# Gather indices four groups ahead and four buffers of gathered rows in the last layer's edge loop

## The chip, the cores and the metric

The program runs on one core of a Trainium2 chip. The metric is the device time of one execution in microseconds (us), the median of several runs. The core has five engines with an instruction queue each: PE (TensorE, matrix products), DVE (VectorE), ACT (ScalarE), POOL (GpSimd, which here issues the indirect transfers) and SP (SyncE, which issues plain transfers). They meet through semaphores: an instruction raises one when it has finished, another queue waits until it has reached a value.

## The reference

Four graph layers run on 3125 nodes of 256 features with 53125 edges: an attention layer, a message-passing layer of five rounds, a mean over neighbours, and last the layer that the change touches (`_L3_gnn_ref`):

```python
row, col = (edge_indices[0], edge_indices[1])
edge_in = jnp.concatenate([h[row], h[col], edge_attr], axis=-1)
msg = jax.nn.relu(edge_in @ W1.T + b1) @ W2.T + b2
agg = jax.ops.segment_sum(msg, row, num_segments=h.shape[0])
...
h_new = (1.0 - z) * n + z * h
```

The kernel splits `W1` by columns: one part multiplies `h[row]`, one `h[col]`, one the edge attributes. The first two are made once for each node, so that for an edge only a sum of three terms is left, a ReLU, and a sum over the edges of a node (`W2` is folded into later weights).

## The kernel before

The last layer's edge loop works on groups of 4 x 128 edges; `GL = SL // 4` = 110 groups. Edges are sorted by source node, so the source term of a group comes by one-hot products from `row_parts` in SBUF. The `col` term comes from DRAM: `col_dram` holds one row of 256 floats for each node, and POOL gathers 128 rows with each of four `indirect_dma_start` (L2100), whose indices stand in `m_idx`. Groups alternate between two halves of each buffer (q = 0 and 1): `m_idx`, `col_rows`, `m_msg`, `p_pre`, `m_hotT`, `attrT`. `m_ends` and `m_attrs` have four slots and come by SP from `rec_dram`.

What each queue does for group g, in the order of the code:

- SP, `load_over(g)` (L2080): waits for the index copy, the local numbers and the turned attributes of group g - 4, then issues the two loads (L2075, L2076).
- DVE, `work(g)`: `choose(g + 2)` (local numbers L2206, one-hots `turn_hot` L2211); `sum_parts(g + 1)` (L2219 on: waits for the rows of g + 1, `rows_in`, and for PE's `pre_done`; two adds L2223 of `col_rows` and `p_pre` into `m_msg`; raises `pre_added`); `add_sums(g)` (four adds of `p_sum` into `agg_sum` L2232, between them `sum_hot` of the next group L2215).
- PE, in a pair: `products(g + 1)` (L2128 and L2132 into `p_pre`, raises `pre_done`), `turn(g + 2)` (transposes L2117, raises `attrT_ps`, and L2121), `add_up(g)` (L2143 into `p_sum`, waits for ACT's `msg_ready`).
- ACT: `finish(g)` (ReLU L2181, waits for `pre_added`), then `prepare(g + 2)`: the index copy L2171, the copy of `attrT` L2175, which waits for PE's `attrT_ps` and `pre_done`, and the copy of `m_hotT` L2177.
- POOL, `gather(g + 2)`: waits for that index copy (`idx_ready`) and for `sum_parts(g)` (`pre_added`), whose buffer it writes over.

The queues are written out by hand, with no scheduler. The order of each is the order of the calls.

Of the kernel before, what the change touches and what calls it, by code (L numbers as in the profile page):

```python
# [9 lines left out]
I32 = mybir.dt.int32  # L10
# [120 lines left out]
def program(nc, a, out):  # L131
# [9 lines left out]
    with top:  # L141
        def sb(name, shape, dt, ctx=top):
            return ctx.enter_context(nc.sbuf_tensor(name, shape, dt))
# [1795 lines left out]
        with ExitStack() as ctx:  # L1939
# [9 lines left out]
            with ExitStack() as inner:  # L1949
# [93 lines left out]
                idx = [sb(f"m_idx{q}", [P, 4], I32, inner) for q in range(2)]  # L2043
                col_rows = [sb(f"col_rows{q}", [P, 4, D], F32, inner) for q in range(2)]
# [14 lines left out]
                rows_in = [sem(f"e_rows_in{q}") for q in range(2)]  # L2059
# [9 lines left out]
                with nc.Block() as block:  # L2069
# [23 lines left out]
                    @block.gpsimd  # L2093
                    def _(pool):
                        def gather(g, q):
                            pool.wait_ge(idx_ready, g + 3)
                            pool.wait_ge(pre_added, g + 1)
                            pool.nop().then_inc(waits_passed, 1)
                            for u in range(4):
                                nc.gpsimd.indirect_dma_start(  # L2100
                                    col_rows[q][:, u, :], None, col_dram,
                                    bass.IndirectOffsetOnAxis(ap=idx[q][:, u:u + 1].bitcast(U32), axis=0)).then_inc(rows_in[q], 16)

                        def pair_of(i):
                            gather(i * 2, 0)
                            gather(i * 2 + 1, 1)
                        looped(pool, GL // 2, pair_of)
# [56 lines left out]
                    def _(act):  # L2164
                        act.nop().then_inc(idx_ready, 2)

                        def prepare(g, q, i, slot, n):
                            act.wait_ge(ends_in[slot], n * 16 + 16)
                            if i is not None:
                                act.wait_ge(rows_in[q], i * 64)  # L2170
                            nc.scalar.copy(idx[q][:], ends[slot][:, :, 0:1].rearrange("p u o -> p (u o)")).then_inc(idx_ready, 1)  # L2171
                            act.wait_ge(attrT_ps, g + 3)
                            if i is not None:
                                act.wait_ge(pre_done, g - 1)
                            nc.scalar.copy(attrT[q][:], p_attrT[:])  # L2175
                            act.wait_ge(hotT_ps, g + 1)
                            nc.scalar.copy(hotT[q][:], p_hotT[:]).then_inc(turned_sb, 1)  # L2177
# [5 lines left out]
                        def pair_of(i, slot, n):  # L2183
                            finish(i * 2, 0)
                            prepare(i * 2 + 2, 0, i + 1, slot, n)
                            finish(i * 2 + 1, 1)
                            prepare(i * 2 + 3, 1, i + 1, slot + 1, n)

                        prepare(0, 0, None, 0, 0)
                        prepare(1, 1, None, 1, 0)  # L2190
                        two_pairs(act, pair_of)
# [4 lines left out]
                    def _(dve):  # L2196
# [20 lines left out]
                        def sum_parts(g, q, i):  # L2217
                            dve.wait_ge(rows_in[q], i * 64 + 64)
# [3 lines left out]
                            for v in range(2):  # L2222
                                r = TT(msg[q][:, 2 * v:2 * v + 2, :], col_rows[q][:, 2 * v:2 * v + 2, :], p_pre[q][:, 2 * v:2 * v + 2, :], ALU.add)  # L2223
# [14 lines left out]
                        def work(g, q, i, tiles, slot, n):  # L2238
                            choose(g + 2, q, i + 1, slot, n)
                            sum_parts(g + 1, 1 - q, i + q)  # L2240
# [12 lines left out]
                        sum_parts(0, 0, 0)  # L2253
                        two_pairs(dve, pair_of)
                        tiles = read_registers(nc, by_src_table, SL - 8, 8, ET.DVE, NT - 1)
                        sum_parts(GL - 1, 1, GL // 2 - 1)
# [200 lines left out]
```

## Time and profile before

| | |
|---|---|
| median of 3 runs | 4330.24 us (4321.47 to 4361.82) |
| profiled execution, its time | 4346.08 us |
| profiled execution, its span | 4344.2 us |
| last layer's edge loop, first load to last add | 3346.67 to 4173.15 us of the span |
| PE busy there (3366 to 4157 us) | 631.09 of 791.00 us |
| DVE, ACT, POOL busy there | 487.86, 217.66, 405.43 us |
| mean granted TensorE clock over the span | 0.859 |

Busy time is the sum of an engine's instructions without those that only wait, move registers or issue plain transfers. The execution's own time lies 1.88 us over its span, and the profiled execution 15.84 us over the median of the three runs.

### The profile page before, as it was taken

Reading aid. Unit: us, or ns where it says so; the run is one execution under the profiler, and the core shown is the slowest. Engines: PE = TensorE matmul, PEld = TensorE weight load, DVE = VectorE, ACT = ScalarE, POOL = GpSimd, SP = SyncE. Lnnn points to the kernel's source line nnn. Section 1 sums busy time; section 2 is a strip of 40 time slices with the busy share of each in tenths; the row PEclk is TensorE's granted clock in tenths of the full one; section 3 lists DMA queues with packets and bytes.
Section 4 is the critical chain, followed back from the end, with each engine's and each line's share of the span. In section 5 each row is a group of like instructions: output and inputs, shape, how many; then the busy total and the mean of one; then the engine's idle time right before and its main releaser. Section 6 shows DMA issues by size and latency. Waiting matters only on the chain. (4 is left out here: it accounts for less than half of the span.)

```text
span 4344.2 us, 64735 instructions
## 1 busy us (share of the span) xinstructions
PE 3493.5 (80%) x16068; PEld 2303.3 (53%) x16069; DVE 2472.1 (57%) x7800; ACT 1066.5 (25%) x2559; POOL 2135.9 (49%) x1867
## 2 busy tenths in 40 slices
PE   6377777777887777669898989897896888787878
PEld 4245555555655555435454555554555555455544
DVE  8756777777777777662222222213555666566668
ACT  0121222222222222132121222211544222222222
POOL 0366788787888888304444444420001555545510
PEclk9877777777777777779999999998898999999989
DMA  7258565665555556223434444431232333333320
GB/s 255 45 136 283 133 136 132 135 135 132 137 133 138 137 134 138 53 70 125 157 115 154 130 134 135 134 104 47 74 118 57 93 92 88 88 87 89 89 59 21
DMA packets 490706, 505.18 MB, mean 116 GB/s; under 512 B 225327, under 2 KB 395789, under 8 KB 490523
## 3 DMA queue, kind: packets, MB, share of 16 engines
q0 software_dynamic: 141664, 236.21, 22.7%
q1 hardware_dynamic: 336238, 248.00, 20.0%
q10 hardware_dynamic: 12749, 20.33, 1.3%
q8 instruction: 23, 0.38, 0.0%
q14 instruction: 32, 0.26, 0.0%
HBM read 433.87 MB, written 70.48 MB: 116 GB/s over the span
## 5 line engine op out<-in xcount | busy, mean ns | idle before, releaser
L1039 PE MATMUL p_out<-rows,hot 128*128 128x266 f32 x2048 | 828.6, 559 | 33.0 <-DVE rows L1161 25.6
L964 POOL DMA_INDIRECT count_dram<-number,place x384 | 653.8, 1703 | 164.7 <-issue 121.2
L1573 POOL DMA_INDIRECT rec_dram<-records,edge_place x416 | 408.4, 982 | 515.1 <-PE p_hi L1615 232.6
L1039 PEld LDWEIGHTS p_out<-rows,hot 128*128 128x128 f32 x2048 | 522.7, 275 | 229.3 <-DVE rows L1161 104.6
L2100 POOL DMA_INDIRECT col_rows<-col_dram,m_idx x440 | 417.9, 950 | 454.3 <-ACT m_idx L2171 313.9
L956 POOL DMA_INDIRECT rows<-att_dram,idx x512 | 550.6, 1075 | 163.3 <-issue 139.9
L1503 PE MATMUL p_hi<-cbuf,parts 128*128 128x400 f16 x1750 | 582.7, 333 | 2.9 <-issue 2.8
L1502 PE MATMUL p_lo<-cbuf,parts 128*128 128x400 f16 x1750 | 583.2, 333 | 2.3 <-issue 2.3
L1531 DVE TENSOR_TENSOR node_sum<-p_hi,low_sb 128x400 f32<-128x400 f32 x80 | 46.0, 574 | 656.1 <-ACT low_sb L1522 623.9
L1161 DVE TENSOR_TENSOR rows<-rows 128x512 f32<-128x512 f32 x512 | 351.1, 686 | 0.2 <-ACT rows L930 0.2
L1022 PE MATMUL p_top<-rhs,hot 128*128 128x17 f32 x1024 | 185.3, 318 | 174.1 <-DVE rhs L1100 159.6
L2128 PE MATMUL p_pre<-attr_w,attrT 128*128 128x512 f32 x440 | 242.4, 634 | 45.4 <-ACT m_hotT L2177 45.4
L1022 PEld LDWEIGHTS p_top<-rhs,hot 128*128 128x128 f32 x1024 | 172.0, 254 | 192.7 <-DVE rhs L1100 176.5
L2232 DVE TENSOR_TENSOR agg_sum<-agg_sum,p_sum 128x256 f32 x440 | 185.1, 421 | 151.9 <-remote 78.0
L1502 PEld LDWEIGHTS p_lo<-cbuf,parts 128*128 128x128 f16 x1750 | 171.4, 98 | 148.1 <-issue 23.3
L907 ACT COPY scores<-rows 128x64 f32<-128x64 f32 x128 | 39.3, 307 | 855.3 <-DMA rows<-att_dram,idx 855.3
L2143 PE MATMUL p_sum<-m_msg,sum_hot 128*128 128x256 f32 x880 | 244.1, 426 | 4.1 <-DVE sum_hot L2215 4.1
L1503 PEld LDWEIGHTS p_hi<-cbuf,parts 128*128 128x128 f16 x1750 | 171.5, 98 | 132.2 <-issue 13.0
L2132 PEld LDWEIGHTS p_pre<-row_parts,m_hotT 128*128 128x128 bf16 x1320 | 132.9, 101 | 147.9 <-issue 135.7
L2223 DVE TENSOR_TENSOR m_msg<-col_rows,p_pre 128x512 f32<-128x512 f32 x220 | 141.2, 683 | 119.9 <-remote 52.6
L1522 ACT ACTIVATE low_sb<-p_lo 128x400 f32<-128x400 f32 x80 | 40.3, 504 | 650.8 <-PE p_hi L1504 603.5
L1978 POOL MEMSET attr_w<- 128x512 f32 x1 | 0.5, 525 | 399.0 <-POOLq L365 399.0
(394 smaller groups left out, 6247.5 us busy)
## 6 DMA issues: line engine op xcount, KB each, us to landing
cbuf<-count_dram SPq DMA_DIRECT2D x40, 2500.0 KB
dl_rep<-dl_dram SPq DMA_DIRECT2D x128, 256.0 KB
count_dram<-zeros SPq DMA_DIRECT2D x20, 1000.0 KB, 21.2
g_rows<-count_dram SPq DMA_DIRECT2D x25, 800.0 KB, 4.2
rec_dram<-blank ACTq DMA_DIRECT2D x1, 17600.0 KB
records<-in_edges POOLq DMA_DIRECT2D x32, 520.0 KB
key_rep<-key_dram SPq DMA_DIRECT2D x64, 256.0 KB
m_attrs<-rec_dram SPq DMA_DIRECT2D x110, 128.0 KB
```

What stands on the lines that cost most here:

```text
L956: nc.gpsimd.indirect_dma_start(rows[r][:, u, :], None, att_dram, bass.IndirectOffsetOnAxis(ap=idx[r][:, u:u + 1].bitcast(U32), axis=0)).th ...
L964: nc.gpsimd.indirect_dma_start(count_dram, bass.IndirectOffsetOnAxis(ap=place[r][:, n, c:c + 1].bitcast(U32), axis=0), number[r][:, 2 * n ...
L1022: m = nc.tensor.matmul(p_top[:, u, :], hot[r][:, u, :], rhs[:, u, :], start=True, stop=True)
L1039: m = nc.tensor.matmul(p_out[q][:, side, 0:HALF], hot[k][:, u, :], rows[k][:, u, side * HALF:(side + 1) * HALF], start=(u == 0), stop=(u = ...
L1161: TT(row[:, :, 0:HEAD - 1], row[:, :, 0:HEAD - 1], row[:, :, HEAD - 1:].broadcast_to([P, HW, HEAD - 1]), ALU.mult).then_inc(msg_ready, 1)
L1502: nc.tensor.matmul(p_lo[m][:], parts[:, k, m, 1, :], cbuf[q][:, k, :], start=(k == 0), stop=(k == NT - 1))
L1503: nc.tensor.matmul(p_hi[m][:], parts[:, k, m, 0, :], cbuf[q][:, k, :], start=(k == 0), stop=False)
L1573: nc.gpsimd.indirect_dma_start(rec_dram, bass.IndirectOffsetOnAxis(ap=edge_place[:, at:at + 1].bitcast(U32), axis=0), records[b % 3][:, j, ...
L2100: nc.gpsimd.indirect_dma_start(col_rows[q][:, u, :], None, col_dram, bass.IndirectOffsetOnAxis(ap=idx[q][:, u:u + 1].bitcast(U32), axis=0) ...
L2128: nc.tensor.matmul(p_pre[q][:, 2 * v:2 * v + 2, :].rearrange("p u d -> p (u d)"), attrT[q][:, v, :], attr_w[:].rearrange("p k d -> p (k d) ...
L2143: r = nc.tensor.matmul(p_sum[v][:, u, :], sum_hot[q][:, 2 * v + u, :], msg[q][:, 2 * v + u, :], start=True, stop=True)
L2232: TT(own, own, p_sum[u // 2][:, u % 2, :], ALU.add).then_inc(added, 1)
```

## The change

ACT no longer makes the indices of group g + 2 within `prepare(g + 2)`. A new function `index` makes them from four buffers: four at the start, and from then on two at the head of each pair, those of groups g + 4 and g + 5, before `finish(g)`. POOL's `gather(g + 4)` waits for its indices and for `sum_parts(g)`; `col_rows` and `m_idx` have four buffers, with a semaphore for each of the four. DVE's `sum_parts` reads the buffer of its slot. PE and SP keep their queues.

```diff
-                idx = [sb(f"m_idx{q}", [P, 4], I32, inner) for q in range(2)]
-                col_rows = [sb(f"col_rows{q}", [P, 4, D], F32, inner) for q in range(2)]
+                idx = [sb(f"m_idx{q}", [P, 4], I32, inner) for q in range(4)]
+                col_rows = [sb(f"col_rows{q}", [P, 4, D], F32, inner) for q in range(4)]
...
-                rows_in = [sem(f"e_rows_in{q}") for q in range(2)]
+                rows_in = [sem(f"e_rows_in{q}") for q in range(4)]
...
-                        def gather(g, q):
-                            pool.wait_ge(idx_ready, g + 3)
-                            pool.wait_ge(pre_added, g + 1)
-                            pool.nop().then_inc(waits_passed, 1)
+                        def gather(g, slot):
...
+                        def gather_over(g, slot):
+                            pool.wait_ge(idx_ready, g + 3)
+                            pool.wait_ge(pre_added, g - 1)
+                            pool.nop().then_inc(waits_passed, 1)
+                            gather(g, slot)
+
+                        for g in range(4):
+                            pool.wait_ge(idx_ready, g + 3)
+                            gather(g, g)
...
-                        def prepare(g, q, i, slot, n):
+                        def index(slot, n, fresh=False):
                             act.wait_ge(ends_in[slot], n * 16 + 16)
-                            if i is not None:
-                                act.wait_ge(rows_in[q], i * 64)
-                            nc.scalar.copy(idx[q][:], ends[slot][:, :, 0:1].rearrange("p u o -> p (u o)")).then_inc(idx_ready, 1)
+                            if not fresh:
+                                act.wait_ge(rows_in[slot], n * 64)
+                            nc.scalar.copy(idx[slot][:], ends[slot][:, :, 0:1].rearrange("p u o -> p (u o)")).then_inc(idx_ready, 1)
+
+                        def prepare(g, q, i):
...
-                        def pair_of(i, slot, n):
+                        def pair_of(i):
                             finish(i * 2, 0)
-                            prepare(i * 2 + 2, 0, i + 1, slot, n)
+                            prepare(i * 2 + 2, 0, i + 1)
...
+                        def both(j):
+                            for half in range(2):
+                                index(2 * half, j + 1)
+                                index(2 * half + 1, j + 1)
+                                pair_of(j * 2 + half)
...
-                        def sum_parts(g, q, i):
-                            dve.wait_ge(rows_in[q], i * 64 + 64)
+                        def sum_parts(g, q, slot, n):
+                            dve.wait_ge(rows_in[slot], n * 64 + 64)
```

On ACT, in the loop's body, the order of one pair before (the branch and the register rows are the sequencer's; L2181 is the ReLU, L2171 the index copy):

```order
L2181 ACTIVATE m_msg<-m_msg 128x1024
L2168 ISA
L2170 ISA
L2171 COPY m_idx<-m_ends 128x4
L2172 REGISTER_ALU
L2174 REGISTER_ALU
L2175 COPY attrT<-p_attrT 128x256
L2177 COPY m_hotT<-p_hotT 128x512
L2180 REGISTER_ALU
L2181 ACTIVATE m_msg<-m_msg 128x1024
L2171 COPY m_idx<-m_ends 128x4
```

The same place on ACT after (L2178 is now the index copy, L2190 the ReLU, L2184 and L2186 the copies of `attrT` and `m_hotT`):

```order
L2177 REGISTER_ALU
L2178 COPY m_idx<-m_ends 128x4 x2
L2189 ISA
L2190 ACTIVATE m_msg<-m_msg 128x1024
L2181 REGISTER_ALU
L2183 REGISTER_ALU
L2184 COPY attrT<-p_attrT 128x256
L2186 COPY m_hotT<-p_hotT 128x512
L2189 REGISTER_ALU
L2190 ACTIVATE m_msg<-m_msg 128x1024
```

Two index copies stand together ahead of the pair's first ReLU, where one stood behind each ReLU.

On POOL, from the start of the block through the loop before (each `x4` is one group's four gathers):

```order
L2100 DMA col_rows<-col_dram,m_idx 128x256 x8
L115 UNCONDITIONAL_BRANCH
L115 ISA
L2097 REGISTER_ALU
L2100 DMA col_rows<-col_dram,m_idx 128x256 x4
L2096 REGISTER_ALU
L2097 REGISTER_ALU
L2100 DMA col_rows<-col_dram,m_idx 128x256 x4
```

and after:

```order
L2097 DMA col_rows<-col_dram,m_idx 128x256 x16
L2110 UNCONDITIONAL_BRANCH
L2110 ISA
L2103 REGISTER_ALU
L2097 DMA col_rows<-col_dram,m_idx 128x256 x4
L2102 REGISTER_ALU
L2097 DMA col_rows<-col_dram,m_idx 128x256 x4
```

Four groups are gathered before the loop instead of two; the loop then gathers one group at a time, as before, four ahead of the sum that frees its buffer.

## Rows read from the trace of the kernel before

**Rows 1.** The page, head, section 1 and groups of section 5

```profile
span 4344.2 us, 64735 instructions
...
PE 3493.5 (80%) x16068; PEld 2303.3 (53%) x16069; DVE 2472.1 (57%) x7800; ACT 1066.5 (25%) x2559; POOL 2135.9 (49%) x1867
...
L2100 POOL DMA_INDIRECT col_rows<-col_dram,m_idx x440 | 417.9, 950 | 454.3 <-ACT m_idx L2171 313.9
```

**Rows 2.** Busy time of each engine in three stretches of the edge loop

```profile
core 0: us, PE busy (x) PEld busy (x) DVE busy (x) ACT busy (x) POOL busy (x), PEclk, DMA share, GB/s
3349.00:3366.00 17.00, 10.74 (x41) 5.92 (x42) 4.33 (x20) 3.05 (x7) 9.60 (x10) 0.73 0.51 111
3366.00:4157.00 791.00, 631.09 (x3218) 427.18 (x3215) 487.86 (x1605) 217.66 (x429) 405.43 (x428) 0.94 0.36 89
```

**Rows 3.** Line L2175, ACT's copy of attrT: what ended its waits

```profile
L2175 ACT COPY attrT<-p_attrT x110: 372/373/374, 3350.4 to 4156.9; 128x256 f32<-128x256 f32 x110
its engine sat idle before it (us, times) until:
  DMA g_rows<-count_dram: 313.8, 43
  PE p_attrT L2117: 168.1, 56
```

**Rows 4.** Timeline of ACT, one pair of groups

```profile
3712.09 0.37 ACT L2175 COPY attrT<-p_attrT 128x256 f32<-128x256 f32 x1 [7.65 <-DMA g_rows<-count_dram]
...
3713.46 1.06 ACT L2181 ACTIVATE m_msg<-m_msg 128x1024 f32<-128x1024 f32 x1 [0.52 <-DVE m_msg L2223]
3714.43 0.18 ACT L2171 COPY m_idx<-m_ends 128x4 int32<-128x4 int32 x1
...
3718.72 1.06 ACT L2181 ACTIVATE m_msg<-m_msg 128x1024 f32<-128x1024 f32 x1
3719.69 0.18 ACT L2171 COPY m_idx<-m_ends 128x4 int32<-128x4 int32 x1
3727.03 0.37 ACT L2175 COPY attrT<-p_attrT 128x256 f32<-128x256 f32 x1 [7.16 <-DMA g_rows<-count_dram]
```

**Rows 5.** Timeline of POOL, the same pair

```profile
3715.46 0.95 POOL L2100 DMA_INDIRECT col_rows<-col_dram,m_idx  x1 [5.32 <-ACT m_idx L2171]
...
3720.72 0.96 POOL L2100 DMA_INDIRECT col_rows<-col_dram,m_idx  x1 [0.56 <-issue]
...
3724.49 0.95 POOL L2100 DMA_INDIRECT col_rows<-col_dram,m_idx  x1 [0.31 <-issue]
```

**Rows 6.** Timeline of the same pair: PE, DVE and SP

```profile
3712.14 1.29 DVE L2223 TENSOR_TENSOR m_msg<-col_rows,p_pre 128x512 f32<-128x512 f32 x2 [3.20 <-PE p_sum L2143]
...
3717.41 1.28 DVE L2223 TENSOR_TENSOR m_msg<-col_rows,p_pre 128x512 f32<-128x512 f32 x2
...
3722.24 0.82 PE L2132 MATMUL p_pre<-row_parts,m_hotT 128*128 x6
...
3723.33 1.95 PE L2143 MATMUL p_sum<-m_msg,sum_hot 128*128 128x256 f32 x8
...
3727.08 1.29 DVE L2223 TENSOR_TENSOR m_msg<-col_rows,p_pre 128x512 f32<-128x512 f32 x2 [4.09 <-remote]
3727.25 0.37 SPq L2075 DMA_DIRECT2D m_ends<-rec_dram  x1
```

**Rows 7.** Timeline, a pair whose first gather was followed by a pause

```profile
3757.16 1.28 DVE L2223 TENSOR_TENSOR m_msg<-col_rows,p_pre 128x512 f32<-128x512 f32 x2 [4.22 <-remote]
...
3763.66 0.95 POOL L2100 DMA_INDIRECT col_rows<-col_dram,m_idx  x1 [2.23 <-issue]
...
3771.18 0.95 POOL L2100 DMA_INDIRECT col_rows<-col_dram,m_idx  x1 [0.30 <-issue]
...
3773.76 1.28 DVE L2223 TENSOR_TENSOR m_msg<-col_rows,p_pre 128x512 f32<-128x512 f32 x2 [5.95 <-remote]
```

**Rows 8.** Timeline of a pair without the long wait, ACT and POOL

```profile
3434.00 1.06 ACT L2181 ACTIVATE m_msg<-m_msg 128x1024 f32<-128x1024 f32 x1
...
3436.01 0.95 POOL L2100 DMA_INDIRECT col_rows<-col_dram,m_idx  x1 [1.20 <-issue]
...
3446.66 1.06 ACT L2181 ACTIVATE m_msg<-m_msg 128x1024 f32<-128x1024 f32 x1
```

**Rows 9.** Timeline at the start of the loop: the first load and index copy

```profile
3346.67 0.37 SPq L2075 DMA_DIRECT2D m_ends<-rec_dram  x1
...
3348.59 0.19 ACT L2171 COPY m_idx<-m_ends 128x4 int32<-128x4 int32 x1 [4.16 <-DMA m_ends<-rec_dram]
```

More of the change, by code:

```diff
@@ L2094, in _ @@
                     def _(pool):
-                        def gather(g, q):
-                            pool.wait_ge(idx_ready, g + 3)
-                            pool.wait_ge(pre_added, g + 1)
-                            pool.nop().then_inc(waits_passed, 1)
+                        def gather(g, slot):
                             for u in range(4):
                                 nc.gpsimd.indirect_dma_start(
[L2101 to L2107, printed above, removed]
+                                    col_rows[slot][:, u, :], None, col_dram,
+                                    bass.IndirectOffsetOnAxis(ap=idx[slot][:, u:u + 1].bitcast(U32), axis=0)).then_inc(rows_in[slot], 16)
+                        def gather_over(g, slot):
[6 more added lines that the diff above has]
+                            gather(g, g)
+                        with pool.Fori(1, GL // 4) as j:
+                            for slot in range(4):
+                                gather_over(j * 4 + slot, slot)
+                        for g in range(GL // 4 * 4, GL):
+                            gather_over(g, g % 4)
                     @block.tensor
@@ L2181, in finish @@
                             nc.scalar.activation(msg[q][:], msg[q][:], ACT.Relu).then_inc(msg_ready, 1)
-                        def pair_of(i, slot, n):
+                        def pair_of(i):
                             finish(i * 2, 0)
-                            prepare(i * 2 + 2, 0, i + 1, slot, n)
+                            prepare(i * 2 + 2, 0, i + 1)
                             finish(i * 2 + 1, 1)
[L2187 to L2191, printed above, removed]
+                            prepare(i * 2 + 3, 1, i + 1)
+                        def both(j):
[3 more added lines that the diff above has]
+                                pair_of(j * 2 + half)
+                        for slot in range(4):
+                            index(slot, 0, True)
+                        prepare(0, 0, None)
+                        prepare(1, 1, None)
+                        looped(act, (GL // 2 - 1) // 2 - 1, both)
+                        last = (GL // 2 - 1) // 2 - 1
+                        index(0, last + 1)
+                        index(1, last + 1)
+                        pair_of(last * 2)
+                        pair_of(last * 2 + 1)
                         finish(GL - 2, 0)
@@ L2239, in work @@
                             choose(g + 2, q, i + 1, slot, n)
-                            sum_parts(g + 1, 1 - q, i + q)
+                            sum_parts(g + 1, 1 - q, (slot + 3) % 4, n - 1 if slot == 0 else n)
                             add_sums(g, q, tiles, True)
@@ L2252, in _ @@
                         r.then_inc(sum_hot_ready, 1)
-                        sum_parts(0, 0, 0)
+                        sum_parts(0, 0, 0, 0)
                         two_pairs(dve, pair_of)
                         tiles = read_registers(nc, by_src_table, SL - 8, 8, ET.DVE, NT - 1)
-                        sum_parts(GL - 1, 1, GL // 2 - 1)
+                        sum_parts(GL - 1, 1, (GL - 1) % 4, (GL - 1) // 4)
                         add_sums(GL - 2, 0, tiles[0:4], True)
```

2 lines of the change are left out of this document (1 added, 1 removed).

## The prediction

> **What bounds the kernel now.** I read the page first: the whole program spans 4344.2 us, and 440 gathers of line L2100 cost POOL 417.9 us, with 454.3 us of idle time before them, most of it put down to ACT's index copy [rows 1]. That is the wait the change moves, but an idle POOL costs nothing by itself. So I next read the stretches of the edge loop. Over 791 us PE is busy 631, DVE 488, POOL 405, ACT 218 [rows 2]. No engine is full: 160 us pass in which even PE stands still, and they are the most that any change of order can give back there. 428 gathers in those 791 us are 107 groups, 7.39 us each.
>
> Then I looked for who waits, and on whom. ACT's copy of `attrT` waits 43 times, 313.8 us in all, until something that the view names "DMA g_rows" [rows 3]. That name belongs to an earlier stage whose semaphore number is used again. By the code the copy waits only for PE's signals `attrT_ps` and `pre_done`. The mean of those waits is 313.8 / 43 = 7.3 us. One of them, followed through a pair of groups, shows the period. `sum_parts` starts at 3712.14 and 3717.41, and the next only at 3727.08 [rows 6]: 5.27 and 9.67 us, 14.94 for two groups, which is 7.47 a group and so the loop's mean. The long one is the problem. PE's matmuls for it are recorded from before 3722.24 to 3723.06, and the sums after it to 3725.28 [rows 6], yet ACT, DVE and SP, each of which needs a signal of PE, go on together at 3727.03, 3727.08 and 3727.25 [rows 4, 6]. The signals of PE came some 4 us after its recorded work. In those 4 us only POOL was still busy: its last gather issue ends at 3724.49 + 0.95 = 3725.44 [rows 5], and the release comes 1.64 us later, about what the last rows need to land.
>
> Is that chance? A pair with a disturbed gather answers it. There POOL paused for 2.23 us after a first gather, its last issue ended at 3771.18 + 0.95 = 3772.13, 14.97 us after the `sum_parts` at 3757.16, where the ordinary pair has 3725.44 - 3712.14 = 13.30. The next release, at 3773.76, came 16.60 us after 3757.16 instead of 14.94 [rows 7, 4 to 6]. The gather was 1.67 us late and the release 1.66 us. So the release follows the end of two batches of gathers that run back to back. I read it as the chain: sum_parts (1.29), ReLU start at 3713.46, index copy at 3714.43, first gather at 3715.46, eight gathers to 3725.44, release at 3727.08. Where the second batch begins after a pause of 1.20 us instead of 0.56, the long wait is missing: two groups then take 3446.66 - 3434.00 = 12.66 us from ReLU to ReLU [rows 8, 5].
>
> **The change part by part.**
>
> *Index copies leave the path from the sum to the gather.* Now the first gather starts 3715.46 - 3712.14 = 3.32 us after `sum_parts`. After the change the indices are there long before, and what is left is the sum itself, 1.29 us, and POOL's own path from the signal to the first gather. The nearest row for that path is the one from the end of the index copy, 3714.43 + 0.18 = 3714.61, to 3715.46: 0.85 us. So the gather starts 2.14 us after `sum_parts`, 1.18 us earlier. The second batch starts at the later of 3717.41 + 1.28 + 0.85 = 3719.54 and the end of the first batch; the first batch then begins at 3714.28 and takes 5.26 us to the next start as now (3720.72 - 3715.46), so 3719.54. It is again 1.18 us earlier than 3720.72. The whole back-to-back run moves up by 1.18 us, and with it the release: 14.94 becomes 13.76 us for such a pair. POOL has no more to do than before, 440 gathers of 950 ns.
>
> *How many pairs.* The long wait stands 43 times in 110 groups, near one in each pair. 43 x 1.18 = 51 us. For the other pairs I take nothing: their gathers end before anyone waits.
>
> *Four buffers.* `sum_parts(g)` can no longer wait for its own rows, which were asked for four groups earlier. In the trace this wait hardly shows by its own name, so I price it at nothing. Its upper bound is in the rival in which the long wait vanishes.
>
> *ACT's two index copies ahead of the ReLU.* They are 0.18 us each, as many as before, but now stand behind a wait for `ends` of group g + 5, whose load SP issues only when group g + 1 has been turned. In the pair shown that load goes out at 3727.25 [rows 6]. The first load of the loop takes 3348.59 - 3346.67 = 1.92 us to the copy that needs it [rows 9], so the second copy starts at 3729.17 and the ReLU at 3729.35, against 1.32 us after the sum's start (as 3713.46 after 3712.14), that is 3728.40. The ReLU is 0.95 us late. Queued behind it are the copies of `attrT` and `m_hotT`, and PE's sum over the messages waits for it. In the row pair PE starts that sum at 3723.33, where the ReLU had ended at 3718.72 + 1.06 = 3719.78: 3.55 us of cover, so 0.95 costs nothing. Without cover it would be 0.95 x 55 pairs = 52 us.
>
> *Start and end.* Before the first `prepare` ACT now waits for four loads instead of one: up to the fourth index copy, three more loads at about 1.1 us each, some 3 us once (an estimate from SP's issues; it is no more than 0.1% of the time). At the end the last gather is no longer waited for, a gain of the same order. I leave both out of the sum and let the range hold them.
>
> *Sum.* 4346.08 - 51 = 4295 us for the profiled execution, and the same 51 us from the median: 4330 - 51 = 4279 us, 1.2% less.
>
> *A rule against it.* The rows show a release that moves with the gathers by 1.66 for 1.67 us [rows 7]. The Trainium skill, page "SBUF — State Buffer", section "Who interferes with whom", says that a DMA never contends with a compute engine. Taken strictly, gathers into SBUF could not hold back PE, the shift of 1.18 us would be worth nothing, and the time would stay at 4330 us. The disturbed pair speaks against that reading; it is the third case below.
>
> **The rivals.**
>
> *The long wait vanishes: 4235 us.* If it needs not only gathers in flight but the rows of the very group, or a second batch that starts less than about 1.2 us after the first, then the earlier start and the spare buffers may free PE altogether. Then 43 pairs go from 14.94 to the 12.66 us of the undisturbed one [rows 8]: 43 x 2.28 = 98 us, 4232 us; I say 4235. For it: a pause of 1.20 us already sufficed once. Against: gathers and PE both move up, and two groups of gathers still take 10 us of a 13 us pair, so they will still touch.
>
> *No change: 4330 us.* The pair has a period of its own (PE's work, or what delays its signals whatever the gather does), and the gather follows it. For: the skill's rule above, and that every other engine is also in step with the period, so cause and effect are hard to tell apart. Against: the pair with the paused gather, one case.
>
> *Slower: 4447 us.* Today only every second group is held, because the batch after a release starts 3.3 us later, with a gap behind it. With gathers allowed four ahead, a batch is in flight at each of PE's `pre_done`, and each group may be held to the end of its own batch. The place is the release in every group; the price for a group is 2.14 us to the first gather, 4.71 of issue (3715.46 to 3720.17 by four gathers 1.25 apart, from 0.95 + 3 x 1.25), and 1.64 to the release: 8.5 instead of 7.47, times 110 is 113 us, 4443 us, with some loss at the start 4447. It decides from the point at which the second group of a pair, too, is held for more than the 3.2 us by which an uncovered period of 5.27 falls short of 8.5. Against it: the second batch is the last thing in flight when the long wait ends, so after a release the queue is empty, as today.
>
> *The change does not do what it says* only if the waits on `ends` keep the indices late. The index copies would then stand within a microsecond of the gather, and the result is near the third case.
>
> **How the numbers follow.** The forecast (release moved up by 1.18 us in 43 pairs) has a chance of 0.40; its own range is 4255 to 4305, for 0.6 to 1.8 us in place of 1.18. The long wait gone or mostly gone: 0.25. No change: 0.20. Slower by one way or another, the group-by-group hold first: 0.15. The time is that of the likeliest, 4279. For 8 times in 10 the range takes in the freed loop and no change with the runs' own spread, and leaves out the slow case and the far end of the fast one: 4200 to 4345. A difference of less than 1% (43 us) is about what a measurement of this kernel can't tell from no change. Faster by over 1% means below 4287: some 0.27 of the forecast's 0.40, and nearly all of the freed 0.25, together 0.51. Slower by over 1% is 0.14. The rest, 0.35, is within 1%.
>
> **What the changed profile would show.** The first gather of a pair starts about 2.1 us after a `sum_parts`, not 3.3; POOL's idle time is put down to DVE's `m_msg`, not to ACT's `m_idx`. The long waits of ACT's `attrT` copy are still near 43, but the pair is near 13.8 us. If they are gone, the first rival holds; if the pair is still 14.9 with the gathers done earlier, the second; if nearly every group waits, the third. The loop from the first load to the last add takes some 775 us instead of 826. I am wrong if the release turns out to follow something else, such as the loads of SP or PE's own pace, that happened to shift with the paused gather.

## The result and the profile after

The changed kernel takes 4385.67 us (median of 4 runs, 4368.93 to 4390.07), the kernel before 4325.85 us beside it (4 runs). The ratio is 1.0114, with a 95% interval of 1.0084 to 1.0143: slower by 1.1%, where 1.2% faster was forecast. On the chip, the kernel before shows one of two levels by occasion, near 4130 or near 4350 us, so every ratio here compares runs of one occasion; the result above and the profile of before belong to the upper one.

The page of the changed kernel, head, section 1 and the gathers' group:

```profile
span 4382.0 us, 64576 instructions
...
PE 3494.9 (80%) x16068; PEld 2300.1 (52%) x16069; DVE 2465.7 (56%) x7800; ACT 1065.7 (24%) x2559; POOL 2129.2 (49%) x1867
...
L2097 POOL DMA_INDIRECT col_rows<-col_dram,m_idx x440 | 417.9, 950 | 473.7 <-ACT m_idx L2178 208.6
```

No engine does more than before [rows 1], and the gathers take the same 950 ns. All of the loss is waiting. Nearly all of it lies in the edge loop: from its first load to SP's first load behind the loop (`m_wh`) it takes 859.6 us (3350.90 to 4210.50) where before it took 827.0 (3346.67 to 4173.65). That is 32.6 of the 37.8 us between the two spans. It comes in two pieces. The first `sum_parts` of the loop's body, that of group 1, starts 29.7 us after the first load instead of 20.0 (+9.8). From there to group 109 it takes 822.3 instead of 797.9 us (+24.3), 7.61 us a group instead of 7.39. The end gives 1.5 us back. The start repeats in later profiles. The second piece is not clear of the scatter between single profiles: another profile of the kernel before (r0 below) takes 822.5 us for the same stretch.

ACT's copy of `attrT` (now L2184), its waits over the whole loop, against [rows 3]:

```profile
L2184 ACT COPY attrT<-p_attrT x110: 366/372/374, 3358.4 to 4197.8; 128x256 f32<-128x256 f32 x110
its engine sat idle before it (us, times) until:
  PE p_attrT L2124: 240.9, 62
  DMA g_rows<-count_dram: 186.6, 35
```

The long waits have become fewer, 35 instead of 43, and shorter, 186.6 / 35 = 5.3 us instead of 7.3. A reader who looked at this view alone would expect a faster loop. DVE's adds show the other side. In the list of waits of the stretch 3400 to 4150 us they stand in these two rows, where the same stretch of before has 73.8 us in 33 waits in the first, and 58.4 in 59 in the second:

```profile
engine line waited for: us in total, times, longest us
...
DVE agg_sum L2254 <- remote: 143.6, 48, 7.3
...
DVE agg_sum L2254 <- PE p_sum L2150: 51.5, 61, 2.4
```

So part of the wait has moved from the sum of the parts to the adds over the messages. One way in which that costs time shows in the timeline of two groups in the steady loop (start, duration, engine, line; in brackets the idle time ahead and what ended it):

```profile
3727.49 1.95 PE L2150 MATMUL p_sum<-m_msg,sum_hot 128*128 128x256 f32 x8
...
3731.12 0.95 POOL L2097 DMA_INDIRECT col_rows<-col_dram,m_idx  x1 [0.30 <-issue]
...
3733.57 0.42 DVE L2254 TENSOR_TENSOR agg_sum<-agg_sum,p_sum 128x256 f32 x1 [4.50 <-remote]
...
3733.63 0.95 POOL L2097 DMA_INDIRECT col_rows<-col_dram,m_idx  x1 [0.30 <-issue]
...
3734.28 0.38 PE L2124 MATMUL p_attrT<-ident,m_attrs 128*128 128x128 f32 x2
3736.43 0.42 DVE L2254 TENSOR_TENSOR agg_sum<-agg_sum,p_sum 128x256 f32 x1 [1.67 <-remote]
3736.50 0.37 ACT L2184 COPY attrT<-p_attrT 128x256 f32<-128x256 f32 x1 [4.46 <-DMA g_rows<-count_dram]
...
3738.04 0.74 DVE L2233 TENSOR_SCALAR turn_hot<-iota_bf,m_local 128x128 bf16<-128x128 bf16 x4
...
3738.69 1.28 DVE L2245 TENSOR_TENSOR m_msg<-col_rows,p_pre 128x512 f32<-128x512 f32 x2
3738.84 0.61 PE L2128 MATMUL p_hotT<-ident_bf,turn_hot 128*128 128x128 bf16 x4 [4.17 <-DVE turn_hot L2233]
```

Before, the hold found PE with all its work for the next group recorded, the turned one-hots included, and ACT, DVE and SP then went on together [rows 4, 6]. Here the signals for `p_sum`, whose matmuls are recorded to end at 3729.44, are among the late ones. DVE stands at its adds until 3733.57 and again until 3736.43; behind them in its queue stand the one-hots `turn_hot` (3738.04), and PE has sat idle for 4.17 us when it gets them. The release at 3736.43, 1.85 us after the last gather's issue ended (3733.63 + 0.95), does not start the next group; a round through DVE, PE and ACT comes after it.

### The profile page after: what moved, and what is told of

The parts are those of the page before. It is cut to its first block and busy times, and to the rows that moved or that the text cites. A ratio compares the mean times of both kernels' runs of the same rounds, so it can differ in the third digit from the quotient of the medians.

```text
span 4382.0 us, 64576 instructions
## 1 busy us (share of the span) xinstructions
PE 3494.9 (80%) x16068; PEld 2300.1 (52%) x16069; DVE 2465.7 (56%) x7800; ACT 1065.7 (24%) x2559; POOL 2129.2 (49%) x1867
## 3 DMA queue, kind: packets, MB, share of 16 engines
q1 hardware_dynamic: 336238, 248.00, 19.6%
## 5 line engine op out<-in xcount | busy, mean ns | idle before, releaser
L2150 PEld LDWEIGHTS p_sum<-m_msg,sum_hot 128*128 128x128 f32 x880 | 179.6, 215 | 29.2 <-issue 2.6
```

What stands on the lines that cost most here:

```text
L2150: r = nc.tensor.matmul(p_sum[v][:, u, :], sum_hot[q][:, 2 * v + u, :], msg[q][:, 2 * v + u, :], start=True, stop=True)
```

## The experiments

All runs are of one core. The late signals of the table are taken from the moments at which semaphores changed, which the trace holds too: of PE's 550 signals in the loop, they are those whose semaphore changes for the first time, at or after the recorded end of the matmul that raises it, 1 to 12 us behind that end. The kernel before has 240 of them, 212 of these within 7 us. The expectations below speak of 233 within 7 us, by a matching that they do not give. Changes that fall together are recorded once (199 for the 220 signals of `p_sum` in the kernel before), so these totals are good to some tens. "Start" is the time from the first load to `sum_parts(1)`; "a group" is the distance of the starts of `sum_parts(10)` and `sum_parts(100)` divided by 90.

| run | level: before | time (ratio, 95%) | loop us | start | a group | late |
|---|---|---|---|---|---|---|
| before | upper: 4325.85 | | 827.0 | 20.0 | 7.43 | 240 |
| changed | upper: 4325.85 | 4385.67 (1.0114, 1.0084 to 1.0143) | 859.6 | 29.7 | 7.73 | 217 |
| r1 changed again | upper: 4364.64 | 4401.09 (1.0082, 1.0053 to 1.0110) | 864.4 | 32.5 | 7.68 | 224 |
| r2 changed, third | upper: 4333.28 | 4371.15 (1.0078, 1.005 to 1.0106) | 864.4 | 30.8 | 7.65 | 228 |
| r0 before again | upper: 4364.64 | 4354.86, one run | 848.3 | 18.2 | 7.65 | 222 |
| e9 no gathers | upper: 4350.83 | 4156.51, one run | 618.3 | 20.0 | 5.48 | 3 |
| e10 one of four | upper: 4333.28 | 4125.96 (0.951, 0.9473 to 0.9547) | 617.3 | 18.7 | 5.48 | 2 |
| k1 plain rows | upper: 4344.18 | 4121.77, one run | 616.3 | 16.7 | 5.48 | 0 |
| e2 no gathers | lower: 4130.09 | 4113.77 (0.9974, 0.9952 to 0.9997) | 615.2 | 16.7 | 5.48 | 1 |
| e3 one of four | lower: 4130.09 | 4118.11 (0.9966, 0.9953 to 0.9979) | 612.9 | 14.6 | 5.48 | 0 |
| e4 plain rows | lower: 4130.09 | 4123.74 (0.9985, 0.9971 to 0.9999) | 614.0 | 14.3 | 5.48 | 0 |
| e6 no gathers | lower: 4134.85 | 4120.27, one run | 614.7 | 16.7 | 5.47 | 0 |
| e7 plain rows | lower: 4134.85 | 4112.65, one run | 613.2 | 14.3 | 5.48 | 0 |
| e1 two ahead | lower: 4130.09 | 4126.89 (0.9992, 0.9974 to 1.0009) | 622.5 | 17.1 | 5.51 | 1 |
| e5 two ahead | lower: 4134.85 | 4137.73 (1.0003, 0.9992 to 1.0015) | 623.6 | 17.0 | 5.51 | 1 |
| e8 two ahead | upper: 4350.83 | 4390.78 (1.0079, 1.0052 to 1.0106) | 855.5 | 19.6 | 7.72 | 228 |
| h2 after the ReLU | upper: 4347.71 | 4399.46 (1.0125, 1.0088 to 1.0163) | 869.8 | 18.0 | 7.80 | 293 |
| h3 copies behind the ReLU | upper: 4347.71 | 4375.67 (1.0077, 1.0039 to 1.0114) | 864.8 | 17.9 | 7.77 | 234 |
| j1 four in turn | upper: 4344.18 | 4340.92 (0.9996, 0.997 to 1.0022) | 803.6 | 19.5 | 7.24 | 229 |
| j2 buffers unused | upper: 4344.18 | 4337.39 (0.999, 0.9967 to 1.0014) | 826.6 | 18.7 | 7.44 | 205 |

The four upper profiles that keep the order of before (before, r0, j1, j2) have loops of 803.6 to 848.3 us, the six with a moved order 855.5 to 869.8. From `sum_parts(1)` to `sum_parts(109)`, without the start, the two sets touch: 775.9 to 822.5 us and 822.2 to 842.9. The loop of one kernel moves by some 20 us from profile to profile, so the loss is read from the ratios of many executions, and the profiles serve for sets and for the start. The work ahead of the loop varies too, whatever the edit: the first load comes between 3325 and 3371 us. That is 38 of the 42 us by which the span of e9 is longer than that of e2; their loops take 618.3 and 615.2 us.

**Is it the gathers that hold PE's signals?** Three edits of the kernel before take them away in different ways. The first leaves out all but the first two groups' gathers; the sums then use old rows:

```diff
+ if is_first(g) or (isinstance(g, int) and g == 1):
      for u in range(4):
          nc.gpsimd.indirect_dma_start(...)
- act.wait_ge(rows_in[q], i * 64)
+ act.wait_ge(rows_in[q], 64)
- dve.wait_ge(rows_in[q], i * 64 + 64)
+ dve.wait_ge(rows_in[q], 64)
```

> The kernel before without the gathers of groups 2 to 109 (the rows of the first two groups are used again and again, so the output is another). Theory A: no signal of PE comes late, ACT's long waits on attrT vanish, and a group takes PE's own 5.4 to 6.0 us: 110 x (7.4 - 5.7) = 190 us less, 4120 to 4180 us. Theory B, and the rival of the prediction that the loop has its own period: the loop keeps some 7.4 us a group, 4310 to 4335 us.

> The kernel before without the gathers of groups 2 to 109. On a chip on which the kernel before takes over 4300 us, theory A: 4110 to 4140 us, the same as on the other chip (4114), with no late signal of PE. If the signals of PE are late there for another reason: 4300 us or more.

> The kernel before without the gathers of groups 2 to 109. At the upper level of the kernel before (over 4300 us), theory A: some 4110 to 4140 us with no late signal of PE. If PE's signals are late at that level for a reason other than the gathers: 4300 us or more.

The second keeps one gather of four:

```diff
- for u in range(4):
+ few = not (is_first(g) or (isinstance(g, int) and g == 1))
+ for u in range(1 if few else 4):
```

> The kernel before with one of a group's four gathers (the rows of u = 1 to 3 stay those of the first pair). Theory A: at most one gather is in flight at a time and a quarter of the time, so nearly all of the gain of leaving all out is there, 4120 to 4200 us. If a single gather in flight already held PE's signals to its end, some 1.5 us a group would be lost, 4250 to 4300 us. Theory B: 4310 to 4335 us.

> The kernel before with one of the four gathers of a group left out three times: after the first two groups only the first of four is issued, and the sums use old rows for the other three. At the lower level it was within 0.4% of the kernel before. At the upper level: if late signals need gathers in flight at the moment of the signal, 4.4 us less of them a group frees most of the loop: 4130 to 4200 us. If each group's first gather is enough to hold PE until it has landed, a hold of about 2 us a group stays: 4200 to 4300 us. If the hold depends on the count of gathers in no way, it stays at 4350 us.

The third puts a plain load of 128 consecutive rows in the place of each gather, from the same queue into the same buffer:

```diff
- nc.gpsimd.indirect_dma_start(col_rows[q][:, u, :], None, col_dram, ...).then_inc(rows_in[q], 16)
+ nc.gpsimd.dma_start(col_rows[q][:, u, :], col_dram[u * P:(u + 1) * P, :]).then_inc(rows_in[q], 16)
```

> The kernel before with each indirect gather replaced by a plain transfer of the same size from POOL's queue, always of the first 512 rows of col_dram (so the output is another). If it is the bytes in flight that hold PE's signals, nothing changes: 4310 to 4340 us and some 40 long waits of ACT. If it is what an indirect gather does apart from its bytes (its descriptors, its single rows of 1 KB), the long waits go: 4130 to 4200 us.

> The kernel before with each indirect gather replaced by a plain transfer of the same size from POOL's queue. On a chip on which the kernel before takes over 4300 us: if bytes in flight from POOL's queue hold PE's signals, over 4300 us too; if it is the indirect form or the scattered rows, 4120 to 4200 us.

> The kernel before with each indirect gather replaced by a plain transfer of the same size from POOL's queue; at the lower level it took 4113 and 4124 us. At the upper level: if bytes in flight from POOL's queue hold PE's signals, over 4300 us; if it is the indirect form or the scattered rows, 4120 to 4200 us.

At the lower level the gathers are worth nearly nothing: without them 4113.77 for 4130.09 us. At the upper level the same edit takes 4156.51 for 4350.83, and both others come to 4126 and 4122 us. In each of them PE's late signals are gone. The stretch 3390 to 3940 us, which lies within the loop in both kernels, of k1 at the upper level:

```profile
core 0: us, PE busy (x) PEld busy (x) DVE busy (x) ACT busy (x) POOL busy (x), PEclk, DMA share, GB/s
3390.00:3940.00 550.00, 540.42 (x3009) 378.73 (x3008) 453.38 (x1506) 203.94 (x401) 213.28 (x400) 1.00 0.47 119
```

And the same stretch of the changed kernel:

```profile
3390.00:3940.00 550.00, 424.82 (x2130) 285.69 (x2129) 320.07 (x1066) 145.12 (x283) 271.14 (x286) 0.92 0.34 86
```

k1 moves more in the same time, 119 for 86 GB/s at a DMA share of 0.47 for 0.34, and none of its signals is late. The packets of one transfer are the same in both traces (32 of 4 KB, a mean of some 212 ns each, and 16 of 4 bytes, 9 ns). What differs is the form: k1's transfers are direct and read consecutive rows, and they keep POOL busy for less time (213.28 us for 400 of them, 0.53 each, against 0.95). So the bytes alone do not hold PE's signals. It is the indirect form, with POOL's longer work on it, or the scattered rows; these were not tried apart. e10 shows that the amount matters: with one gather of four, 2 signals are late, not a quarter of 240.

Where in a run of gathers the hold falls can be counted in the traces. Take gathers with pauses under 0.7 us as one run, and sort PE's signals by the gather that had last begun at their recorded end. In the kernel before, 2 of 46 are late at a run's first gather, 32 of 117 at the second, 52 of 100 at the third, 62 of 129 at the fourth, and 72 of 73 at the fifth to seventh; of the 46 that end over 2 us after an issue, none is. So the hold needs gathers that follow each other, and it is not there at once. Nor does it always last to the end of the run: 23% of the late signals in the kernel before, and 31% in the changed one, come through while a gather is still being issued.

**Is it the distance of four groups?** The changed kernel with its gathers back at two groups ahead, all else kept:

```diff
- pool.wait_ge(pre_added, g - 1)
+ pool.wait_ge(pre_added, g + 1)
...
  for g in range(4):
      pool.wait_ge(idx_ready, g + 3)
+     if g >= 2:
+         pool.wait_ge(pre_added, g + 1)
      gather(g, g)
```

> The changed kernel with its index copies as they are, four groups ahead at the head of a pair, but with POOL's gather of group g waiting for sum_parts(g - 2) as in the kernel before, not for sum_parts(g - 4). Theory A (PE's signals are held back while gathers are in flight, and the change put gathers in flight at more of them): the gathers are again placed as before, 1.2 us earlier after each sum, so the time goes back to the kernel before or under it, 4280 to 4335 us. Theory B (the loss is ACT's: two index copies and a wait for the loaded ends stand ahead of the ReLU): the time stays with the changed kernel, 4370 to 4395 us.

> The changed kernel with POOL's gather of group g waiting for sum_parts(g - 2) again, as timed before on a chip on which the kernel before took 4130 us and no signal of PE was late. Wanted is a chip on which the kernel before takes over 4300 us. Theory A (where the gathers are in flight decides): back to the kernel before or under it, ratio 0.985 to 1.003. Theory B (ACT's order decides): as the changed kernel, ratio 1.008 to 1.012.

> The changed kernel with POOL's gather of group g waiting for sum_parts(g - 2) again. The kernel before has shown two levels, 4130 and over 4300 us, on one and the same chip, so the level belongs to the occasion and not to the chip. Should this be the upper level, theory A (where the gathers are in flight decides): ratio 0.985 to 1.003. Theory B (ACT's order decides): 1.008 to 1.012. At the lower level both give a ratio of 1.000.

Twice at the lower level it equals the kernel before (0.9992, 1.0003); at the upper one it loses as much as the whole change (1.0079). The four groups are not needed for the steady loss. What they make is the start: 29.7 to 32.5 us in the three profiles of the changed kernel, 19.6 here. This timeline of the changed kernel has it:

```profile
3364.11 0.39 PE L2128 MATMUL p_hotT<-ident_bf,turn_hot 128*128 128x128 bf16 x4
...
3365.51 1.28 DVE L2245 TENSOR_TENSOR m_msg<-col_rows,p_pre 128x512 f32<-128x512 f32 x2 [9.75 <-PE p_pre L2139]
...
3367.52 0.37 ACT L2184 COPY attrT<-p_attrT 128x256 f32<-128x256 f32 x1 [8.30 <-DMA g_rows<-count_dram]
...
3369.59 0.71 SPq L2075 DMA_DIRECT2D m_ends<-rec_dram  x1
...
3372.22 0.95 POOL L2097 DMA_INDIRECT col_rows<-col_dram,m_idx  x1 [0.30 <-issue]
...
3374.57 0.59 ACT L2186 COPY m_hotT<-p_hotT 128x512 bf16<-128x512 bf16 x1 [6.68 <-DMA step_dram<-table_i]
...
3375.21 2.08 PE L2135 MATMUL p_pre<-attr_w,attrT 128*128 128x512 f32 x2 [10.71 <-issue]
```

PE's transposes into `p_hotT` end at 3364.50 as recorded, and for the next 10.71 us PE has nothing. Sixteen gathers go out without a pause until 3372.22 + 0.95 = 3373.17. ACT, which has waited for that one signal since 3367.89, goes on at 3374.57, 1.40 us later. This is a clear view of the hold: from 3367.89 on only POOL issues gathers and SP its two loads, and no engine computes. The hold is not on all signals alike, though: amid the same gathers PE's earlier ones, for `p_pre` and `p_attrT`, came through, and DVE went on at 3365.51 and ACT at 3367.52. PE pays once more after it, since its two matmuls take 2.08 us where the same line takes 1.02 in the steady loop; after the 10.71 us without work the clock granted over 3374 to 3380 us is a mean 0.55 of 2.4 GHz, near the lower of its two levels (1.2 GHz), against 1.00 from 3380 to 3400.

**The changed kernel again, and the kernel before as a run of its own**, unaltered:

> The changed kernel as it is, timed again. The kernel before took 4130 us beside the last four kernels, with no late signals of PE in the traces of its variants, where its first profile had 4346 us and 233 late ones. Theory A (the loss is PE's signals, held back while gathers are in flight): where the signals are not held, the change has nothing to lose or give, 4120 to 4140 us beside 4130 for the kernel before; where they are, 4370 to 4395 beside 4330. Theory B (the loss is ACT's order, whatever the signals do): 1% over the kernel before in either state, 4170 beside 4130.

> The kernel before as it is, once more, for a trace beside these runs. Theory A: at 4130 us the loop takes 5.5 us a group and hardly a signal of PE is over 1 us late; at 4330 us it takes 7.4 and some 230 are. Theory B has nothing to say on it.

> The changed kernel once more, unaltered. The kernel before has two levels by occasion, near 4130 and near 4350 us. If the loss needs signals of PE that come late, it must be there at the upper level (ratio 1.008 to 1.014, as in its two timings so far) and gone at the lower one, but for the start of the loop: there ratio 0.999 to 1.003, with about 5.5 us a group and the first sum at about 20 us from the first load. If the loss lay in the order of the work itself, it would be 30 to 50 us at the lower level too: ratio 1.007 to 1.012.

The loss repeats (1.0082, 1.0078). In the profiles of r1 and r0, of one occasion, all of it that the loop shows is the start (32.5 against 18.2 us); from `sum_parts(1)` to `sum_parts(109)` they take 824.0 and 822.5 us. That single pair does not show the steady loss; the timings of h3 below, which has no longer start, do. The changed kernel itself was timed at the upper level alone; at the lower one only its form with gathers two ahead is known.

**Which half of the edit does it?** From e8, h2 makes each gather wait for the ReLU, so that it starts no earlier than before, with ACT's new order kept:

```diff
- pool.wait_ge(pre_added, g + 1)
+ pool.wait_ge(msg_ready, g - 1)
```

> ACT's queue as in the changed kernel (index copies four ahead at the head of a pair), but POOL's gather of group g waits for the ReLU of g - 2 (msg_ready), which ends 0.1 us before the index copy that it waited for in the kernel before: the gathers start at their old moment. At the upper level, theory C (the earlier start of the gathers makes the loss): ratio 0.997 to 1.003. Theory B (ACT's order makes it): 1.006 to 1.012. At the lower level both give 1.000.

And h3 keeps the earlier gather and puts ACT's index copies back, one behind each ReLU, made for group g + 4:

```diff
  def prepare(g, q, i, slot=None, n=None):
+     if slot is not None:
+         index(slot, n)
...
- index(2 * half, j + 1)
- index(2 * half + 1, j + 1)
- pair_of(j * 2 + half)
+ pair_of(j * 2 + half, 2 * half, j + 1)
```

> ACT's queue in the old order (ReLU, index copy, copies of attrT and m_hotT), but each index copy makes the indices of four groups ahead, and POOL's gather of group g waits only for sum_parts(g - 2): the gathers start 1.2 us earlier than in the kernel before. At the upper level, theory C: 1.006 to 1.012, as the changed kernel. Theory B: 0.985 to 1.003. At the lower level both give 1.000.

Both lose (1.0125 and 1.0077). In h3 the gather starts 2.06 us after the start of `sum_parts` (median of 90 groups) and 3.32 us in the kernel before. Its DVE waits 149.0 us ahead of its adds into `agg_sum` until a release at which no recorded instruction ends (the view's "remote", here PE's late signals), r1 142.8, r2 149.2, e8 166.4, against 73.8, 109.7, 58.0 and 74.7 in the four that keep the old order. PE's signals for `p_sum` show the same. In the four old orders 8 to 13 of them have their recorded end at the first gather of a run, and 0 to 2 of these are late. With the earlier gather (changed, r1, r2, e8, h3) 28 to 40 do, and 8 to 21 are late. So the earlier gather alone brings the pattern that the timeline above shows. Where PE then loses its time is less plain. In the stretch 3400 to 4150 us its idle time ahead of the transposes of `turn_hot` is no longer than before (83.9 to 120.5 us against 112.5 to 139.9). What is longer is its idle time ahead of the products into `p_pre`, 45.0 to 66.1 us against 21.0 to 37.6; by the code they wait for ACT's copies of `attrT` and `m_hotT` and for DVE's sum.

h2 shows another. Its gathers do not stay at their old moment but go to 4.03 us behind the sum (median), since in ACT's new order the ReLU stands behind an index copy that waits for its load. Its timeline:

```profile
3700.42 1.28 DVE L2247 TENSOR_TENSOR m_msg<-col_rows,p_pre 128x512 f32<-128x512 f32 x2 [3.43 <-PE p_sum L2152]
...
3702.67 0.19 ACT L2180 COPY m_idx<-m_ends 128x4 int32<-128x4 int32 x1 [1.35 <-DMA m_ends<-rec_dram]
3702.77 1.06 ACT L2192 ACTIVATE m_msg<-m_msg 128x1024 f32<-128x1024 f32 x1
...
3704.61 0.95 POOL L2097 DMA_INDIRECT col_rows<-col_dram,m_idx  x1 [6.04 <-ACT m_msg L2192]
...
3716.21 1.28 DVE L2247 TENSOR_TENSOR m_msg<-col_rows,p_pre 128x512 f32<-128x512 f32 x2 [5.42 <-remote]
```

The first gather comes 4.19 us after the sum, 0.87 later than in the pair of before, and the pair takes 3716.21 - 3700.42 = 15.79 us, 0.85 more than 14.94 [rows 6]. In this pair the release does follow the gathers, as the prediction had it. So h2 is no clean test of ACT's order by itself, which no run tried with the gathers at their old moment; it shows what ACT's order and later gathers cost together.

**Is it the four buffers?** j1 is h3 with the index copy made for group g + 2 again: four buffers used in turn, order and waits as before. j2 is the kernel before with the four buffers and semaphores only allocated:

```diff
- index(slot, n)
+ index(slot, n, isinstance(n, int) and n == 0)
...
- pair_of(j * 2 + half, 2 * half, j + 1)
+ pair_of(j * 2 + half, 2 - 2 * half, j + half)
```

> The order of ACT's queue and the waits of POOL as in the kernel before (indices two ahead, made behind the ReLU), but the four buffers and semaphores used in turn. If using four buffers in turn is enough for the loss: 1.006 to 1.012 at the upper level. If the loss needs the gathers earlier or ACT's new order: 0.997 to 1.003.

> The kernel before with four m_idx, four col_rows and four semaphores of rows allocated, of which it still uses two: the same instructions, other places in SBUF and other semaphore numbers behind them. Theory D (the places make the loss): 1.006 to 1.012 at the upper level. Theories B and C (when and in which order things are issued): 0.997 to 1.003.

Neither moves the time (0.9996 and 0.999). Buffers, their places in SBUF and the numbers of the semaphores are out. j1 and h3 differ in the group whose indices ACT copies, and so in the moment of the gather (3.31 us after the sum, and 2.06). ACT's waits for the loads ahead of these copies are 4.1 and 5.2 us over the whole loop, so they play no part. The two were timed on different occasions, each beside the kernel before, and their intervals do not meet (0.997 to 1.0022, and 1.0039 to 1.0114).

## Why the prediction was wrong

*"Index copies leave the path from the sum to the gather": right.* 2.14 us from sum to gather was forecast; the median in the changed kernel is 2.10 (before: 3.32). One pair has it at 2.06:

```profile
3715.20 1.28 DVE L2245 TENSOR_TENSOR m_msg<-col_rows,p_pre 128x512 f32<-128x512 f32 x2 [0.64 <-PE p_pre L2139]
...
3717.26 0.95 POOL L2097 DMA_INDIRECT col_rows<-col_dram,m_idx  x1 [1.74 <-issue]
```

The bottom of it was right too: at the upper level the gathers do hold back PE's signals (e9, e10, k1).

*The step that failed is "the whole back-to-back run moves up by 1.18 us, and with it the release: 14.94 becomes 13.76 us".* It took the pair of groups as a rigid block in which only the gathers' end sets the release. That fits the two pairs in which the gathers came later: [rows 7] (1.67 us, release 1.66 us) and the pair of h2 (0.87 us, pair 0.85 us longer). When they came 1.2 us earlier, the time did not fall; it rose (h3 against j1, and the changed kernel three times). Forecast for the loop: 51 us less. Measured: 36 to 60 us more for the whole program in three timings, of which the start is 10 to 14.

What the traces show in its place: a hold falls mostly on signals in the middle and at the end of a run of gathers, and an earlier run meets other signals. PE's signals for `p_sum` are late no oftener (of 220, 94, 83, 89 and 87 times in the four profiles of the old order, 81 to 92 times in the changed kernel, e8 and h3), but 8 to 21 of those at a run's first gather now are, where 0 to 2 were, and DVE waits more for late signals: 142.8 to 166.4 us of its unnamed waits against 58.0 to 109.7. In the timeline above DVE's adds, `turn_hot` and PE's transposes then run after the release instead of inside the hold. In the kernel before, the index copy on the path gave PE's signals a head start of 1.2 us over the gathers. That the lost head start is why the loop lost is argued from these counts and waits, not shown: no run moved one signal of PE alone, and PE's idle time grew at another place than this chain (ahead of `p_pre`).

The evidence for the step was one disturbed pair, and it showed a delay. An advance was inferred from it, and no row showed one.

*"Four buffers: nothing": right* (j1, j2).

*"ACT's two index copies ahead of the ReLU: 0.95 us late, covered": the wait was there, the consequence short.* These rows of the changed kernel have the copy waiting 1.15 us for its load:

```profile
3724.82 0.95 POOL L2097 DMA_INDIRECT col_rows<-col_dram,m_idx  x1 [2.85 <-ACT m_idx L2178]
...
3725.11 0.19 ACT L2178 COPY m_idx<-m_ends 128x4 int32<-128x4 int32 x1 [1.15 <-DMA m_ends<-rec_dram]
3725.21 1.05 ACT L2190 ACTIVATE m_msg<-m_msg 128x1024 f32<-128x1024 f32 x1
```

The ReLU starts 3725.21 - 3721.68 = 3.53 us after the sum, where 1.32 + 0.95 = 2.27 was forecast.

But POOL, which was to wait for DVE's `m_msg` alone, still waits for the index copy in 35 cases, 142.4 us, and for `m_msg` in 25, 77.3 us, in the stretch 3400 to 4150 us. The index copies stand behind the rest of ACT's queue, so when ACT stands behind a late signal of PE, they do too. In this pair the gather comes 3.14 us behind the sum at 3721.68, nearly as late as before. e8 keeps this order, h3 does not, and h3 loses as much as e8 (1.0077, 1.0079), so this order shows no cost of its own.

*"Start and end: some 3 us once": mis-sized.* The start costs 10 to 14 us (29.7, 32.5 and 30.8 against 20.0 and 18.2). The step counted the loads and not the sixteen gathers in a row, under which one of PE's first signals waits. By the mechanism of the prediction itself, that hold could have been seen: more gathers in a row, more to wait for. It is 9.8 of the 32.6 us in the profile; in the timings, e8, which is without it, loses no less (1.0079), so there it can't be told from the scatter.

*The rivals.* The slower one had the direction, but not holds in every group: from group 10 to 100 the changed kernel has 24 distances of 7 to 9 us between sums and 23 of over 9, where both profiles of the kernel before have 12 and 32. The other 43 stay under 7 (46 before). At the place that the price was made for, the period is 3721.68 - 3715.20 = 6.48 us, not 8.5: the sum starts 1.33 us ahead of the release of ACT's copy at 3723.01, and that release comes 1.05 us after the last issue (3721.01 + 0.95), not 1.64. The mean is 7.61, and the loss 60 us in place of the 117 of that rival. No change and the freed loop are both refused at this level. A freed loop does exist, 5.48 to 5.51 us a group, but only without the indirect gathers, with one in four of them, or at the lower level.

*The rule of the Trainium skill* ("SBUF — State Buffer", section "Who interferes with whom": a DMA never contends with a compute engine) would have given no change. Within an instruction the traces agree: a pair of matmuls of `attr_w` takes 1.02 us in the held loop and in the free one. Between engines the measurement decides otherwise: with the indirect gathers 240 of PE's signals come late and the loop takes 827 us, with plain transfers of the same bytes it takes 616.

*What stays open:* by which path the gathers delay PE's signals; whether the form, POOL's longer work on it or the scattered rows matter; how much of the steady loss goes through DVE's adds; and what sets the level of an occasion. One chip showed both levels. At the lower one four indirect gathers a group cost 5.51 - 5.48 = 0.03 us a group (e1 against e2), at the upper one 1.8 to 2.3.

## What to carry to other kernels

A wait that ends in step with some other work may be set by it, but the step may be rigid in one direction only: before moving that work, list who would be waiting for what at the hold's new place, and what is queued behind each. Ask of a transfer that is made early not only when its data is needed but what it does to others while in flight; here a start that filled all buffers at once gave the longest hold. And where a view says that long waits became fewer while the time grew, look for the same signal's other waiters.

## What was not expected of the hardware

- A PE signal can be acted on only 10 us after the recorded end of its matmul (3364.50 to 3374.57) while sixteen indirect gathers are issued. The four releases followed above came 1.05 to 1.85 us after the last issue of a run, but about a quarter of the late signals come through before it.
- The hold builds up within a run of gathers: 2 of 46 signals of PE are late at the first gather, 72 of 73 at the fifth to seventh, and none over 2 us after an issue.
- Of what was tried, only the indirect gathers do it: 440 plain transfers of the same bytes from the same queue leave no such delay (4122 for 4344 us), and neither does a quarter of the gathers (4126 for 4333 us).
- The same program on the same chip has it on one occasion and not on another: 4134.85 and 4364.64 us for the kernel before. Most of the difference lies in this loop: for one kernel, e5 and e8, the loop has 231.9 of the 272.1 us between the spans, the work ahead of it 39.8.
